# Row maxima into two rounded rows by ScalarE, GpSimd and VectorE instead of VectorE alone

## What is computed

```python
q = rope(heads(Wq @ layernorm(x) + bq)); k = rope(heads(Wk @ c + bk)); v = heads(Wv @ c + bv)
p = softmax(q @ k^T / sqrt(16), axis=-1)              # 512 x 512 for each of 8 heads
x = x + tanh(g_xattn) * (Wo @ (p @ v) + bo)
gate_up = layernorm(x) @ dequant_fp4(gate_up_w)^T     # 512 -> 2 x 1408
y = (silu(gate) * up) @ dequant_fp4(down_w)^T
x = x + tanh(g_ffn) * y / rms(y)
```

## Time and profile before

| | |
|---|---|
| median of 3 runs | 838.14 us (835.2 to 841.78) |
| the profiled execution | 833.57 us, span 831.8 us, mean granted TensorE clock 0.93 |
| busy over the span | TensorE 719.3 us, VectorE 622.9, ScalarE 531.9, GpSimd 376.5 |
| attention, steps 0 to 15 | from 59 us to 480 us, steps of 21.6 to 32.4 us |
| step 5, from 190.6 to 215.7 us | 25.1 us: TensorE 24.59 busy, VectorE 22.98, ScalarE 20.79, GpSimd 11.10, clock 1.00 |

### The profile page before, as it was taken

One profiled execution on the slowest core, in us unless ns is written; L12 is line 12 of the kernel. 1 busy time (PEld: TensorE's weight loads), 2 busy tenths in 40 slices (PEclk: granted clock), 3 DMA queues, 4 the chain that ended last, 5 costly groups with the idle time before them and its releaser, 6 DMA issues. The chain is left out here.

```text
span 831.8 us, 13555 instructions
## 1 busy us (share of the span) xinstructions
PE 719.3 (86%) x4660; PEld 338.8 (41%) x4660; DVE 622.9 (75%) x879; ACT 531.9 (64%) x965; POOL 376.5 (45%) x298
## 2 busy tenths in 40 slices
PE   3369999889999999999999805998998999889995
PEld 1124334333334334333344303554554555555553
DVE  5588999979889869898999316766677677776774
ACT  2217888768868658788788805565566457465744
POOL 2123344445444425454401102676558655955662
PEclk9559999999989859999999957999999999999999
DMA  6655677766776666666632140000000200000011
GB/s 212 196 154 164 148 191 199 203 158 179 197 215 184 160 172 172 165 184 183 177 95 63 38 159 36 1 0 2 1 0 26 77 0 1 27 25 1 1 39 63
DMA packets 55113, 88.74 MB, mean 107 GB/s; under 512 B 16901, under 2 KB 20357, under 8 KB 55045
## 3 DMA queue, kind: packets, MB, share of 16 engines
q1 hardware_dynamic: 54320, 87.68, 37.9%
q10 hardware_dynamic: 724, 0.20, 0.1%
HBM read 46.95 MB, written 34.34 MB: 98 GB/s over the span
## 5 line engine op out<-in xcount | busy, mean ns | idle before, releaser
L556 ACT ACTIVATE probs<-st_ps 128x512 f32<-128x512 f32 x512 | 277.2, 595 | 108.9 <-PE st_ps L449 97.9
L699 DVE TENSOR_REDUCE neg_max<-s_ps 128x2 f32<-128x1024 f32 x256 | 303.8, 1214 | 38.3 <-PE s_ps L437 37.7
L1075 POOL TENSOR_TENSOR pair<-parts 128x512 f32<-128x512 f32 x88 | 116.3, 1325 | 135.7 <-ACT parts L1095 135.7
L467 PE MATMUL pv_ps<-probs,v_ones 128*32 128x256 f32 x2048 | 168.9, 403 | 0.8 <-ACT pv_sb L562 0.8
L437 PE MATMUL s_ps<-k_stack,q_stack 48*128 48x512 f32 x512 | 137.3, 533 | 34.5 <-DVE neg_max L699 29.4
L1200 PE MATMUL gu_ps<-x_head,gu_bits 128*128 128x512 f16 x352 | 136.3, 387 | 19.3 <-ACT parts L1095 16.8
L1200 PE MATMUL gu_ps<-x_rest,gu_bits 128*128 128x512 f16 x352 | 135.4, 385 | 0.0
L1095 ACT ACTIVATE parts<-gu_ps,gu_sc 128x512 f32<-128x512 f32 x176 | 111.5, 680 | 10.6 <-PE gu_ps L1200 10.6
L449 PE MATMUL st_ps<-q_stack,k_stack 50*128 50x512 f32 x512 | 112.1, 424 | 0.0
L437 PEld LDWEIGHTS s_ps<-k_stack,q_stack 48*128 48x128 f32 x512 | 50.9, 196 | 148.8 <-DVE neg_max L699 72.5
L962 DVE SCALAR_TENSOR_TENSOR up<-gu_ps,gu_sc,up 128x512 f32<-128x512 f32 x132 | 98.6, 747 | 8.0 <-PE gu_ps L1200 4.2
(11 more groups left out here) (109 smaller groups left out, 816.2 us busy)
## 6 DMA issues: line engine op xcount, KB each, us to landing
q_stack<-image SPq DMA_DIRECT2D x64, 192.0 KB, 3.5
k_stack<-image SPq DMA_DIRECT2D x64, 192.0 KB, 4.5
image<-split_head SPq DMA_DIRECT2D x32, 256.0 KB
image<-split_head SPq DMA_DIRECT2D x64, 128.0 KB
image<-split_rest SPq DMA_DIRECT2D x32, 256.0 KB
ct<-ctx_dram SPq DMA_DIRECT2D x16, 256.0 KB, 6.3
swap<-proj SPq DMA_DIRECT2D x64, 64.0 KB, 2.7
scale_of<-inverse_scratch SPq DMA_DIRECT2D x16, 256.0 KB
```

The source lines that it names most:

```text
L467: last = nc.tensor.matmul(pv_ps[2 * KC * j:2 * KC * (j + 1), cols], v_ones[b % 2][:, kt, j, quad, :], probs[at % PROBS][:, j, cols], start ...
L556: nc.scalar.activation(probs[at % PROBS][:, tile % 4, :], st_ps[item % ST_BANKS][:], ACT.Exp).then_inc(st_read, 1)
L699: nc.vector.tensor_reduce(neg_max[j // 2][:, :, j % 2, qt], s_ps[item % S_BANKS][:], AXIS_X, ALU.max, negate=True).then_inc(s_read, 1)
L1075: nc.gpsimd.tensor_tensor(pair[:, n], parts[T_ % 2][:, 2 * n], parts[T_ % 2][:, 2 * n + 1], ALU.add).then_inc(pairs_ok, 1)
```

## The change

`turn_max` is split in three. The cast goes to ScalarE (`head_max`), after the exps of slot 0 (h = 1) and of slot 7 (h = 0, ahead of L528); each waits for the last reduction of its half. The subtraction goes to GpSimd (`rest_max`): for h = 0 after the rotation and ahead of `rest_pass`, for h = 1 after `scale_heads` and ahead of `scale_down`. The transpose stays on VectorE (`line_max`), after the reduction of slot 1 (h = 1) and of slot 9 (h = 0). The first reduction of a half waits until the subtraction has read the maxima of the batch before. SyncE's order is not touched.

```diff
@@ -41,6 +41,7 @@
 GU_WORDS, DN_WORDS = KT * GU_COLS // 4, IT * T // 4
 BIT_STEPS = 3
 DN_AT, GU_AT = 2, 3
+LINE_AT = 1
 X_GAIN = 2.0 ** 11
 
 SLOTS = 2 * QUADS * KT
@@ -561,6 +562,12 @@
                     act.wait_ge(heads_ok, b - 1)
                 nc.scalar.activation(pv_sb[h][b % 2][:], pv_ps[:], ACT.Copy).then_inc(pv_out[h], 1)
 
+            def head_max(act, n, h):
+                act.wait_ge(s_read, S_NO["score", n, (h + 1) * SLOTS // QUADS - 1] + 1)
+                if n:
+                    act.wait_ge(max_line[h], n)
+                nc.scalar.activation(max_rows[h][:, 0], neg_max[h][:].rearrange("p o j k -> p (o j k)"), ACT.Copy).then_inc(max_head[h], 1)
+
             def gate(act, b):
                 item = ST_NO["mix", b]
                 act.wait_ge(st_full, item + 1)
@@ -579,6 +586,10 @@
                         values_out(act, b, 0)
                     for odd in two:
                         exponential(act, b, 2 * slot + odd)
+                    if slot == 0:
+                        head_max(act, b, 1)
+                    if slot == 7 and b + 1 < B:
+                        head_max(act, b + 1, 0)
                     if slot == MIX_AT and b >= 2:
                         gate(act, b - 2)
                     if slot == ROT_AT and b + AHEAD_PROJ < B:
@@ -610,6 +621,7 @@
                 nc.scalar.activation(keep["gates"][:], pv_ps[:, 2:4], ACT.Tanh).then_inc(gated, 1)
                 nc.scalar.preload_act_table_set("natural_log_exp_and_others")
                 inverse_dev(act, 3)
+                head_max(act, 0, 0)
                 for b in range(B):
                     scalar_step(act, b)
                 values_out(act, B - 1, 1)
@@ -648,6 +660,11 @@
                 if n:
                     engine.wait_ge(st_full, ST_NO["pass", n - 1] + 1)
                 ops.tensor_scalar(xn[:], xt[n % X_TILES][:], neg_mean[:], rstd[:, 1:2], ALU.add, ALU.mult).then_inc(normed, 1)
+
+            def rest_max(pool, n, h):
+                pool.wait_ge(max_head[h], n + 1)
+                nc.gpsimd.tensor_tensor(max_rows[h][:, 1], neg_max[h][:].rearrange("p o j k -> p (o j k)"),
+                                        max_rows[h][:, 0].bitcast(F32), ALU.subtract).then_inc(max_rest[h], 1)
 
             def scale_heads(engine, ops, b):
                 engine.wait_ge(inverse_in, 16 * (b + 1))
@@ -696,15 +713,12 @@
                 item = S_NO["score", n, slot]
                 j, qt = score_of(slot)
                 dve.wait_ge(s_full, item + 1)
+                if n and slot % (SLOTS // QUADS) == 0:
+                    dve.wait_ge(max_rest[j // 2], n)
                 nc.vector.tensor_reduce(neg_max[j // 2][:, :, j % 2, qt], s_ps[item % S_BANKS][:], AXIS_X, ALU.max,
                                         negate=True).then_inc(s_read, 1)
 
-            def turn_max(dve, n, h):
-                dve.wait_ge(s_read, S_NO["score", n, (h + 1) * SLOTS // QUADS - 1] + 1)
-                maximum = neg_max[h][:].rearrange("p o j k -> p (o j k)")
-                nc.vector.tensor_copy(max_rows[h][:, 0], maximum).then_inc(max_head[h], 1)
-                dve.wait_ge(max_head[h], n + 1)
-                nc.vector.tensor_tensor(max_rows[h][:, 1], maximum, max_rows[h][:, 0].bitcast(F32), ALU.subtract).then_inc(max_rest[h], 1)
+            def line_max(dve, n, h):
                 dve.wait_ge(max_rest[h], n + 1)
                 if n:
                     dve.wait_ge(max_out[h], 16 * n)
@@ -740,14 +754,14 @@
                             dve.wait_ge(gu_in, 16 * 2 * KT)
                         piece, step = divmod(slot - 1, BIT_STEPS)
                         turn_nibbles(dve, gu_bits, step, slice(piece * DN_WORDS, (piece + 1) * DN_WORDS), BIT_STEPS * piece, gu_turned)
-                    if slot == 0:
-                        turn_max(dve, b, 1)
+                    if slot == LINE_AT:
+                        line_max(dve, b, 1)
                     if slot == 3 and b + 4 < B:
                         statistics(dve, b + 4)
                     if slot == 6 and b:
                         invert_sums(dve, b - 1)
-                    if slot == 7 and b + 1 < B:
-                        turn_max(dve, b + 1, 0)
+                    if slot == SLOTS // QUADS + LINE_AT and b + 1 < B:
+                        line_max(dve, b + 1, 0)
                     if slot == 7 and proj_n < B:
                         head_pass(dve, proj_n)
                     if slot == 11 and proj_n < B:
@@ -795,8 +809,8 @@
                         statistics(dve, 3)
                     if slot == 3:
                         head_pass(dve, 2)
-                    if slot == 7:
-                        turn_max(dve, 0, 0)
+                    if slot == SLOTS // QUADS + LINE_AT:
+                        line_max(dve, 0, 0)
                     if slot == 11:
                         head_rot(dve, 2)
                 dve.wait_ge(gated, 1)
@@ -818,6 +832,9 @@
                 if proj_n < B:
                     rotate_own(pool, nc.gpsimd, proj_n)
                     rotate_partner(pool, nc.gpsimd, proj_n)
+                if b + 1 < B:
+                    rest_max(pool, b + 1, 0)
+                if proj_n < B:
                     rest_pass(pool, nc.gpsimd, proj_n)
                 if b + 4 < B:
                     normalise(pool, nc.gpsimd, b + 4)
@@ -825,6 +842,8 @@
                     rest_rot(pool, nc.gpsimd, proj_n)
                 if b:
                     scale_heads(pool, nc.gpsimd, b - 1)
+                if b + 1 < B:
+                    rest_max(pool, b + 1, 1)
                 if DN_AT <= b < DN_AT + IT:
                     scale_down(pool, b - DN_AT)
 
@@ -852,7 +871,9 @@
                 rest_pass(pool, nc.gpsimd, 2)
                 rotate_partner(pool, nc.gpsimd, 2)
                 normalise(pool, nc.gpsimd, 3)
+                rest_max(pool, 0, 0)
                 rest_rot(pool, nc.gpsimd, 2)
+                rest_max(pool, 0, 1)
                 for b in range(B):
                     pool_step(pool, b)
                 residual(pool, nc.gpsimd, B - 2)
```

## The result

The changed kernel takes 866.88 us, the median of 4 runs (865.82 to 872.22), where the kernel before took 839.96 in the same comparison. The ratio is 1.0341, with a 95% interval of 1.0275 to 1.0407: slower by 3.4%; between the two medians lie 26.9 us.

A forecast was written before the change was run, and what follows sets the result against it. TensorE bounds the kernel, VectorE nearly a second bound. 1.3 us in each of 12 steps (15.6), less 3 for long steps and 2.4 saved on VectorE, gives +10.2: 843.8, or 848 on the median; range 843 to 856, wide 829 to 867.

The forecast's parts named there:

- the rival of the spreading half clock: TensorE stops at slots 0, 8 and 9; four more steps fall to long ones, 4.6 us each: 866 us, chance 0.15.
- chain C: Next step's k rows, queued behind the h = 0 store, reach TensorE's slot 0 late: 1.0 us a step, range 0.2 to 3.5.
- the slack of 1.6 us: In step 5, k rows land at 212.0 and TensorE's first score starts at 213.61; set against 2.6 us of delay.
- VectorE's 24.1 us would bring nothing: Casts and subtractions leaving VectorE: h = 1 worth nothing, h = 0 saves 0.4 us a step, 0.15 after ScalarE's cost.
- The whole 24.1 us on an engine that never stalls: Rival from the skill's ScalarE rule: all of VectorE's removed 24.1 us comes back, 814 us, chance 0.04.
- L685 inherits the port: VectorE's next cast would meet GpSimd's L631 in the removed cast's place, so the 0.6 us excess stays unsaved.
- The two new operations: 128 x 16 casts on ScalarE taken at 0.25 us, costing 0.25 a step (0.2 to 0.6); GpSimd subtractions at 0.2 us.
- The line 4.7 us behind the reciprocal: SyncE's h = 0 store moves from 2.1 to 4.7 us behind the reciprocal's start, delaying everything queued behind by 2.6 us.
- Chain B: Late reciprocals delay GpSimd's L657 and subtraction; VectorE waits 1.2 us at slot 1's transpose, hidden by projections: cost 0.
- Chain A: SyncE's late queue delays the h = 1 store and gathered sums; step 6's reciprocal wait grows 0.8 us, mean +0.3 a step.
- The signs: Store 4.5 to 5.3 us behind reciprocal; k_stack waits in most steps; reciprocal waits beyond five steps; VectorE 20 us less busy.
- The rival of the recovering clock: Half-clock stretches of the five long steps go away: 7.3 us faster, 831 us, chance 0.19.

The follow-up runs named there:

- experiment 5: Changed kernel plus two throw-away TensorE matmuls (128x512 and 128x256) in slot 0 while the k rows are awaited: 855.83 us, ratio 1.0185.
- Experiment 3: Kernel before, with only load_half(b + 2, 0) issued later, behind load_inverse, store_rest and load_inputs: 875.71 us, ratio 1.0408.
- experiment 7: Changed kernel with only h = 1 made by three engines, h = 0 whole on VectorE after slot 7: 842.85 us, ratio 1.0021.
- experiment 4: Kernel before, with the whole turn_max of h = 0 on VectorE after slot 9 instead of slot 7: 865.08 us, ratio 1.0275.
- experiment 12: Changed kernel with load_half(b + 2, 0) ahead of store_max(b + 1, 0) and both load_max moved back, run again: 822.81 us, ratio 0.9786.

## Why the prediction was right or wrong

The direction was right and the size was not: the forecast was 848, with 843 to 856 as its own range, a rise of 1.2%; measured were 866.88 and 3.4%. The wide range up to 867 holds it only just, by its edge, the rival of the spreading half clock.

- **The step that failed is the price of chain C, and with it the clock behind it at nothing.** The mechanism was right (the line late, the k rows behind it late, TensorE standing at slot 0). The price was 1.0 us a step, half in the long steps. In steps 1 to 12 of the changed kernel the weight loads waited 22.3 us for the k rows, 1.9 a step; the matmuls themselves 16.4. And the sum had nothing for the half clock that follows such a wait: the eight falls behind slot 0 hold 37.4 us at 1.2 GHz. A slot of scores that takes 1.24 us at the full clock (99.24 to 100.47 or 100.47 to 101.71 in the trace) takes 2.09 there (369.66 to 371.75), so an estimate of what these falls cost is 37.4 x (1 - 1.24 / 2.09) = 15 us, 1.3 a step; experiment 5 freed some 16.
- **Why the wait was longer.** Not by the delay: counted from the reciprocal, the first k DMA goes out 6.7 us behind it before and 8.7 after (means of steps 1 to 12), 2.0 us later and not 2.6, since in the steps where the cast met L631 the store had been 3.1 to 3.3 us behind the reciprocal already. It was the landing. TensorE needs both k DMAs, and 4.5 us is the median of all 64 single ones. The rows of one tile give a pair its own numbers: step 5 and step 8 before, step 1 after.

```profile
DMA to landing us min/median/max: 4.3/4.5/4.7
...
DMA to landing us min/median/max: 4.2/5.6/7.0
...
DMA to landing us min/median/max: 4.1/5.0/5.9
```

The slower of the pair took 4.7 to 7.0 us over steps 1 to 12 before, 5.5 on average, and 5.5 again after. Step 5, from which the slack of 1.6 us was read, had the quickest pair of all. The range up to 7.0 was at hand.

- **What follows chain C was priced as a rival of its own**, "four more steps fall", 15%. Its mechanism came true, in seven more steps than before; its 866 hit the measured time, but four steps at 4.6 us on top of a chain C of 1.0 is not what happened, and the hit is partly luck. Steps 3, 4 and 10 fell behind the reciprocal; step 0 was under 1.00 before too; the others fell behind the k rows. Experiment 3 has the k rows as the only cause and loses 4.1%; experiment 5 gives back 1.6 of 3.4 points without touching the lateness of the rows.
- **That VectorE's 24.1 us would bring nothing** fits the runs: 17.4 us less work and no gain, nothing for h = 1 (experiment 7), and no difference to one engine at slot 9 (experiment 4). With the queue in order it stays open (experiment 12).
- **The whole 24.1 us on an engine that never stalls** was misread in the prediction: only the cast, 12.8 us, went to ScalarE; the subtraction, 11.3 us, went to GpSimd, where it took 0.40 to 0.41 us instead of 0.22 when VectorE's cast was held up beside it.
- **That L685 inherits the port** was right, and dearer than said. The cast that had a mean of 392 ns now has 711; seven of the 16 took 0.94 to 1.35 us, one of them in step 3, where it starts at 160.36 and GpSimd's L643 (L631 before) runs to 161.12:

```profile
L702 DVE CAST split_head<-proj 128x512 fp32r<-128x512 f32 x16 | 11.4, 711 | 1.6 <-ACT proj L547 0.9 <-DMA image<-split_rest 0.7
...
L725 DVE STREAM_TRANSPOSE max_lines<-max_rows 128x32 f32<-128x32 f32 x32 | 6.5, 202 | 2.6 <-POOL max_rows L666 2.4
...
L569 ACT ACTIVATE max_rows<-neg_max 128x16 fp32r<-128x16 f32 x32 | 6.9, 217 | 16.7 <-DVE neg_max L718 16.4
...
L666 POOL TENSOR_TENSOR max_rows<-neg_max,max_rows 128x16 fp32r<-128x16 f32 x32 | 8.4, 264 | 34.1 <-ACT max_rows L569 33.9
```

- **The two new operations**: 217 ns on ScalarE (0.25 taken), 264 on GpSimd (0.2 taken). TensorE's waits for exps at L450 are 9.9 us in 21, before 3.5 in 9, some 0.4 us a step, inside the 0.2 to 0.6 that was said.
- **The line 4.7 us behind the reciprocal** was right: 4.2 in steps 1 and 2 (100.92 to 105.11), 4.2 to 5.1 over steps 1 to 12.
- **Chain B** cost nothing, as said, but its wait of 1.2 us a step did not come: VectorE idled 2.6 us in all for the transpose, 2.4 of it for GpSimd, in 6 waits.
- **Chain A**: over the whole span the waits for the gathered sums grew from 18.2 us in 6 to 22.6 in 7, about 0.3 us a step as said. What it left out is the half clock behind the longest of them, as in chain C.
- **The signs**: the store came 4.2 to 5.1 us behind the reciprocal, score loads waited for the k rows in 11 of the steps 1 to 12, the reciprocal waited in six steps of attention where it had in five, and VectorE was 17.4 us less busy where 20 were said.
- **The rival of the recovering clock** did not come: three falls behind the reciprocal stayed where there had been four, and eight behind slot 0 were added.

## What to carry to other kernels

When an operation is moved later, ask what is queued behind its store on the engine that issues the DMAs, and set the slower landing of all that the reader needs against the slack, over many steps, not the median of single DMAs. A new wait of TensorE of some 2 us cost more here than its own length, as in most cases the clock fell behind it; work put into the wait gave back about half of the loss. Before relieving an engine that is 90% busy, look at the order of the DMA queue: here two moves in it gained 1.8% without the split, and the split without them lost 3.4%.

## What the runs showed of the hardware

- A wait of 2.14 us by TensorE in a stream that was otherwise full was followed by some 7 us at 1.2 GHz (granted 1.00, then 0.65 and 0.50, then 1.00 again); with 1.56 us of throw-away matmuls in that place it stayed at 1.00 in the same slots. In the changed kernel 8 of the 11 matmul waits for the k rows from step 0 on, those of 1.43 to 2.80 us without that of 1.73, were followed by 3.4 or 6.8 us at 1.2 GHz; those of 0.49, 1.16 and 1.73 us were not.
- Of two equal DMAs issued 0.4 us apart for the same tile, one took 4.2 us from issue to landing and the other 7.0 (step 8 of the kernel before); the median of all 64 is 4.5.
- A GpSimd subtraction of 128 x 16 takes 0.21 to 0.23 us in most steps and 0.40 to 0.41 in the seven where VectorE's cast of 128 x 512 was held up beside it. A ScalarE copy of 128 x 16 takes 0.21 to 0.22 us throughout, in those seven steps too. The Trainium skill, SBUF — State Buffer, section Who interferes with whom, states that ScalarE never waits for another engine and that the shared port belongs to VectorE and GpSimd; these durations agree.
